# Two-layer graph and expert network on one core: the first layer's expert rows are added into a table in device memory and loaded back in three groups, in place of a table of expert rows and eleven gathers

## The reference, cut to what matters

```python
x = x + graph0(layernorm(x), adj)                 # adj @ (input * W)
x = x + ffn0(layernorm(x))                        # attention, then the first expert layer
x = x + graph1(layernorm(x), adj)                 # attention over the graph, with adj as weights
x = x + ffn1(layernorm(x))                        # second expert layer

# inside ffn0: a normed input x, x = x + attention(x), then with h2 = layernorm(x)
for i in range(8):                                # capacity = ceil(1354 * 1.6 / 8) = 271
    mask = (topk_idx == i).any(-1)                # each token has its two best experts
    sel = first `capacity` tokens of the mask
    yi = gelu(h2[sel] @ w1[i] + b1[i]) @ w2[i] + b2[i]
    out = out.at[sel].set(yi, mode='drop')        # a later expert overwrites an earlier one
return x + out
```

## Time and profile before

| what | value |
|---|---|
| median of three runs | 882.79 us |
| the profiled execution, device time | 877.23 us |
| its span in the profile | 875.4 us |
| TensorE busy | 772.8 us (88%) |
| VectorE busy | 611.6 us (70%) |
| ScalarE busy | 409.9 us (47%) |
| GpSimd busy | 336.2 us (38%) |
| mean granted TensorE clock | 0.944 of full speed |

### The profile page before, as it was taken

One profiled execution on the slowest core, in us unless ns is written; L12 is line 12 of the kernel. 1 busy time (PEld: TensorE's weight loads), 2 busy tenths in 40 slices (PEclk: granted clock), 3 DMA queues, 4 the chain that ended last, 5 costly groups with the idle time before them and its releaser, 6 DMA issues. The chain is left out here.

```text
span 875.4 us, 13715 instructions
## 1 busy us (share of the span) xinstructions
PE 772.8 (88%) x4212; PEld 583.1 (67%) x4213; DVE 611.6 (70%) x1175; ACT 409.9 (47%) x836; POOL 336.2 (38%) x333
## 2 busy tenths in 40 slices
PE   5999888999999999752999992999957999999994
PEld 4997554555555543342999992577846888888883
DVE  6675777766666679984898984687785655666552
ACT  3336344555566556612657552642342454444551
POOL 2700257676666777734252105000002344333332
PEclk9999989999999999985999996999968999999997
DMA  7538776787887777505155402972293287752110
GB/s 270 205 107 323 175 243 230 258 264 250 271 259 257 252 242 233 184 1 200 48 212 176 176 27 62 388 268 92 96 356 102 44 283 230 233 165 37 31 19 0
DMA packets 61623, 159.02 MB, mean 182 GB/s; under 512 B 20875, under 2 KB 39489, under 8 KB 58371
## 3 DMA queue, kind: packets, MB, share of 16 engines
q1 hardware_dynamic: 40627, 97.97, 33.1%
q0 software_dynamic: 20944, 60.38, 22.3%
HBM read 103.00 MB, written 49.93 MB: 175 GB/s over the span
## 5 line engine op out<-in xcount | busy, mean ns | idle before, releaser
L1858 DVE TENSOR_REDUCE mx<-ps 128x1 f32<-128x452 f32 x264 | 148.4, 621 | 68.3 <-PE ps L1314 67.5
L971 ACT ACTIVATE expo<-ps 128x452 f32<-128x452 f32 x264 | 124.5, 551 | 89.7 <-PE ps L1326 88.5
L1334 PE MATMUL ps<-expo,v_st 128*64 128x452 f32 (+1 forms) x576 | 117.3, 529 | 0.0
L1159 ACT ACTIVATE h<-ps,b_l 128x128 f32<-128x128 f32 x224 | 61.0, 384 | 114.6 <-PE ps L1668 111.7
L1314 PE MATMUL ps<-k_st,q_st 96*128 96x452 f32 x264 | 106.0, 413 | 6.8 <-DVE mx L1858 6.5
L1326 PE MATMUL ps<-q_st,k_st 98*128 98x452 f32 x264 | 97.1, 392 | 2.4 <-ACT expo L971 2.3
L905 POOL DMA_INDIRECT out<-y1t,out_row x29 | 46.2, 1592 | 118.2 <-DVE share L2254 94.6
L1314 PEld LDWEIGHTS ps<-k_st,q_st 96*128 96x128 f32 x264 | 50.7, 192 | 53.2 <-DVE mx L1858 36.7
L1685 PE MATMUL ps<-w_ring,h_hi 128*128 x232 | 82.5, 394 | 1.3 <-DVE h_lo L2266 0.5
L837 POOL TENSOR_TENSOR part_lo<-part,part_hi 128x512 fp32r<-128x512 f32 x64 | 80.9, 1289 | 0.5
L2278 DVE COPY h1pre<-ps 128x1024 f32<-128x1024 f32 x29 | 35.5, 1224 | 61.7 <-PE ps L1661 61.6
(11 more groups left out here) (352 smaller groups left out, 1786.3 us busy)
## 6 DMA issues: line engine op xcount, KB each, us to landing
w_l<-w_l SPq DMA_DIRECT2D x8, 2053.0 KB, 8.4
part<-w_l POOLq DMA_DIRECT2D x32, 512.0 KB, 4.9
w_split_d<-part_hi POOLq DMA_DIRECT2D x32, 512.0 KB, 3.8
w_split_d<-part_lo POOLq DMA_DIRECT2D x32, 512.0 KB, 3.7
adj<-adj_t SPq DMA_DIRECT2D x22, 704.0 KB, 4.2
w_ring<-w_split_d SPq DMA_DIRECT2D x10, 1365.5 KB, 7.0
w_ring<-w_split_d SPq DMA_DIRECT2D x5, 1365.0 KB, 6.0
w_ring<-w_split_d SPq DMA_DIRECT2D x1, 4096.0 KB, 13.5
```

The lines of the kernel that those rows point to most:

```text
L971: act.activation(expo[g % 8][:, :], ps[:, 3 + g % 3, 0:QC], ACT.Exp, scale=SCALE).then_inc(s_exp, 1)
L1159: last = act.activation(h1[:, f, :], ps[:, 4 + f // 4, (f % 4) * P:(f % 4 + 1) * P], ACT.Gelu_apprx_tanh, bias=b1_l1[:, bass.ds(e, 1), f])
L1334: return pe.matmul(ps[at:at + 2 * DK, 6 + g // T % 2, lo:hi], v_st[h % 2][:, kt, :], expo[g % 8][:, lo:hi], start=kt < 2, stop=kt == T - 1 ...
L1858: dve.tensor_reduce(mx4[:, n // KB, n % KB:n % KB + 1], ps[:, i % 3, 0:KC], AX_X, ALU.max).then_inc(s_mx, 1)
```

## The change

The sum of residual and u is made before the experts (VectorE, behind `goal0`) and written to a new memory table `x2_d` of 1408 rows. GpSimd adds each expert's rows into that table with three indirect DMAs as soon as ScalarE has copied them, one expert after the other, and tells ScalarE through a new semaphore when a buffer `y0` is free. A list `out_row0` names the destination rows: it comes from `place_of0` with two small instructions, and places without a token point out of range. When all 24 scatters have landed, SP loads `x2_d` back into `x_res` in three DMAs, one for each group, and then the adjacency. The table `ys0_d`, its 16 writes, the eleven gathers, the memset of `nat`, the list `idx` and VectorE's eleven additions are gone. SP no longer waits for an expert's rows between weight loads. TensorE's order is changed: `right(1)` and `left(1)` come before `turn_group(2)`, and `features(0, 2)` behind it.

```diff
 @@ constants and tiles
-GOALS0_READY, ROWS0_NUMBERED, WEIGHTS_READY, GOALS_READY = 1, 2, 3, 4
+GOALS0_READY, WEIGHTS_READY, GOALS_READY = 1, 2, 3
-        idx = place("idx", [T], I32)
+        out_row0 = place("out_row0", [TILES0], I32)
-        x0_d, ys0_d = scratch("x0_d", [P + NP, D]), scratch("ys0_d", [SLOTS0, D])
+        x0_d, x2_d = scratch("x0_d", [P + NP, D]), scratch("x2_d", [NP, D])
-        RIGHT_DONE, LEFT_DONE = (1, 3, 4), (2, 5, 6)
+        RIGHT_DONE, LEFT_DONE = (1, 3, 5), (2, 4, 6)
 @@ SP (behind the write of x0_d, L690)
-            def experts(i, last):
+            sp.wait_ge(s_x2, 1)
+            sp.dma_start(x2_d.rearrange("(t p) d -> p t d", p=P), x_res[:, :, :]).then_inc(s_x2_out, 16)
+
+            with sp.Fori(0, E // 2 - 1) as i:
                 for k in range(2):
                     e = i * 2 + k
-                    if not last:
-                        sp.wait_ge(s_w1lo, e + 1)
-                        sp.wait_ge(s_w2lo, e + 1)
-                        sp.dma_start(w_l0[k][:, :], ...).then_inc(s_w0[k], 16)
-                    sp.wait_ge(s_yo, PRIMED + e + 1)
-                    sp.dma_start(ys0_d[bass.ds(e * CAPP, (CT - 1) * P), :]..., y0[k][:, 0:CT - 1, :]).then_inc(s_ys[k], 16)
-                    sp.dma_start(ys0_d[bass.ds(e * CAPP + (CT - 1) * P, CREM), :], y0[k][0:CREM, CT - 1, :]).then_inc(s_ys[k], 16)
-            with sp.Fori(0, E // 2 - 1) as i:
-                experts(i, False)
-            experts(E // 2 - 1, True)
+                    sp.wait_ge(s_w1lo, e + 1)
+                    sp.wait_ge(s_w2lo, e + 1)
+                    sp.dma_start(w_l0[k][:, :], ...).then_inc(s_w0[k], 16)
+
+            sp.wait_ge(s_ys, 16 * CT * E)
+            for n, (lo, hi) in enumerate(ROW_GROUPS):
+                sp.dma_start(x_res[:, lo:hi, :], x2_d[lo * P:hi * P, :].rearrange("(t p) d -> p t d", p=P)).then_inc(s_x2_in[n], 16)
             sp.wait_ge(s_y0_ps, PRIMED + E)
-            for t in range(T):
-                sp.wait_ge(s_gath[t], 16)
             for j in range(3):
                 sp.dma_start(adj1[j][:, :], adj[j]).then_inc(s_adj1[j], 16)
 @@ GpSimd (behind load_xs0(0) and load_xs0(1))
-            for e in range(2, E):
-                load_xs0(e)
-                if e == ZERO_AT:
-                    pool.memset(nat[:, :, :], 0.0).then_inc(s_gz, 1)
-            pool.wait_ge(s_gz, 1)
-            pool.wait_ge(s_idx, ROWS0_NUMBERED)
-            for k in range(2):
-                pool.wait_ge(s_ys[k], PRIMED + 32 * (E // 2))
-            for t in range(T):
-                pool.indirect_dma_start(
-                    out=nat[:, t, :], out_offset=None, in_=ys0_d[:, :],
-                    in_offset=bass.IndirectOffsetOnAxis(ap=idx[:, t:t + 1], axis=0),
-                    bounds_check=SLOTS0 - 1, oob_is_err=False).then_inc(s_gath[t], 16)
+            def add_rows0(e):
+                pool.wait_ge(s_yo, PRIMED + e + 1)
+                for c in range(CT):
+                    w = P if c < CT - 1 else CREM
+                    at = e * CT + c
+                    pool.indirect_dma_start(
+                        out=x2_d[:, :], out_offset=bass.IndirectOffsetOnAxis(ap=out_row0[0:w, at:at + 1], axis=0),
+                        in_=y0[e % 2][0:w, c, :], in_offset=None, bounds_check=N - 1, oob_is_err=False,
+                        compute_op=ALU.add).then_inc(s_ys, 16)
+
+            for e in range(E):
+                if e + 2 < E:
+                    load_xs0(e + 2)
+                if e == 0:
+                    pool.wait_ge(s_x2_out, 16)
+                else:
+                    pool.wait_ge(s_ys, 16 * CT * e)
+                    pool.sem_inc(s_y_free, 1)
+                add_rows0(e)
 @@ ScalarE, rows_out
-                act.wait_ge(s_ys[k], PRIMED + written)
+                act.wait_ge(s_y_free, PRIMED + added)
 @@ TensorE
             turn_group(1)
+            right(1)
+            left(1)
+            turn_group(2)
             features(0, 2)
-            turn_group(2)
-            right(1)
             right(2)
-            left(1)
             left(2)
 @@ VectorE, before the experts (behind goal0, L1997)
-            slot_numbers(C_OFF)
-            row_number(sa)
+            step(dve.tensor_scalar(beyond0[:, :], place_of0[:, :], 0.0, FAR, ALU.is_equal, ALU.mult))
+            dve.scalar_tensor_tensor(out=out_row0[:, :], in0=place_of0[:, :], scalar=-float(P), in1=beyond0[:, :],
+                                     op0=ALU.add, op1=ALU.add)
+            dve.tensor_tensor(x_res[:, :, :], x_res[:, :, :], u[:, :, :], ALU.add).then_inc(s_x2, 1)
 @@ VectorE, behind the experts
-            dve.tensor_tensor(x_res[:, :, :], x_res[:, :, :], u[:, :, :], ALU.add).then_inc(s_x2, 1)
...
-            dve.wait_ge(s_x2, 1)
             def normed_group(n):
                 lo, hi = ROW_GROUPS[n]
+                dve.wait_ge(s_x2_in[n], 16)
                 for t in range(lo, hi):
-                    dve.wait_ge(s_gath[t], 16)
-                    dve.tensor_tensor(x_res[:, t, :], x_res[:, t, :], nat[:, t, :], ALU.add).then_inc(s_x2, 1)
-                    if t > lo:
-                        dve.wait_ge(s_x2, 1 + t)
-                        dve.bn_stats(stats[:, t - 1, :], x_res[:, t - 1, :])
-                dve.wait_ge(s_x2, 1 + hi)
-                step(dve.bn_stats(stats[:, hi - 1, :], x_res[:, hi - 1, :]))
+                    last = dve.bn_stats(stats[:, t, :], x_res[:, t, :])
+                step(last)
```

More of the change, by code:

```diff
@@ L39 @@
 CREM = CAPP - (CT - 1) * P
-SLOTS0 = E * CAPP
 TILES0 = E * CT
 TILES1 = (2 * N + E * (P - 1)) // P
-GOALS0_READY, ROWS0_NUMBERED, WEIGHTS_READY, GOALS_READY = 1, 2, 3, 4
+GOALS0_READY, WEIGHTS_READY, GOALS_READY = 1, 2, 3
 PAIR_BANKS = (3, 4, 5, 7, 3, 4)
@@ L47 @@
 ZEROED = 48
-ZERO_AT = 4
 B2_BANKS = (3, 3, 4, 4, 5, 5, 6, 6, 1, 1, 2)
@@ L335, in build_program @@
         place_of0 = place("place_of0", [TILES0])
+        beyond0 = place("beyond0", [TILES0])
         assert cursor[0] <= offsets["lg"]
@@ L457, in build_program @@
         s_yo = sem("y0_ready")
-        s_ys = [sem(f"ys0_written{i}") for i in range(2)]
-        s_gz = sem("gather_zeroed")
-        s_gath = [sem(f"rows_gathered{t}") for t in range(T)]
+        s_ys = sem("expert_rows_added")
+        s_y_free = sem("expert_rows_buffer_free")
+        s_x2_out = sem("residual_rows_written")
+        s_x2_in = [sem(f"summed_rows_loaded{n}") for n in range(len(ROW_GROUPS))]
         ROUTER_DONE, BIAS_DONE, WO_TURNED, FOLD_DONE, WAL_DONE, COMB_TURNED = range(1, 7)
@@ L509, in build_program @@
         s_b2 = sem("b2_products_done")
-        s_x2 = sem("two_residuals_added_then_layer0_tile_summed")
+        s_x2 = sem("two_residuals_added")
         s_b2_add = sem("b2_added")
@@ L547, in build_program @@
         PRIMED = 1
-        primed = [s_exp, s_av, s_cr, *s_cout, s_h0, s_hlo, s_y0_ps, s_yt, s_yo_ps, s_yo, *s_ys,
+        primed = [s_exp, s_av, s_cr, *s_cout, s_h0, s_hlo, s_y0_ps, s_yt, s_yo_ps, s_yo, s_y_free,
                   s_g1, s_y1_ps, s_y1, s_ring]
@@ L1031, in _, with rows_out, expert0 @@
             act.activation(std[:, 0:1], ones[:, 0:1], ACT.Gelu)
-            def rows_out(e, k, written):
+            def rows_out(e, k, added):
                 act.wait_ge(s_yo_ps, PRIMED + e + 1)
-                act.wait_ge(s_ys[k], PRIMED + written)
+                act.wait_ge(s_y_free, PRIMED + added)
                 act.activation(y0[k][:, 0:2, :], ps[:, 6, :].rearrange("p (s d) -> p s d", d=D), ACT.Identity)
                 act.activation(y0[k][0:CREM, 2, :], ps[0:CREM, 7, 0:D], ACT.Identity).then_inc(s_yo, 1)
-            def expert0(i, k, first=False, more=True):
+            def expert0(i, k, first=False, reused=True, more=True):
                 e = i * 2 + k
@@ L1047, in expert0 @@
                     if f == YT_AT and not first:
-                        rows_out(e - 1, 1 - k, i * 32 if k else i * 32 - 32)
+                        rows_out(e - 1, 1 - k, i * 2 + k - 2 if reused else 0)
                 if more:
@@ L1058, in _ @@
             expert0(0, 0, first=True)
-            expert0(0, 1)
+            expert0(0, 1, reused=False)
             with act.Fori(1, E // 2 - 1) as i:
@@ L1064, in _ @@
             expert0(E // 2 - 1, 1, more=False)
-            rows_out(E - 1, 1, (E // 2 - 1) * 32)
+            rows_out(E - 1, 1, E - 2)
             def normed_group(n):
@@ L1960, in choose @@
                 step(dve.tensor_tensor(mask[:, :, :], key, over_e(valid), ALU.mult))
[L1962 to L1966, removed]
             for k in range(PARTS_AHEAD):
@@ L1974, in _ @@
             step(dve.tensor_tensor(mask[:, :, :], mask[:, :, :], slot[:, :, :], ALU.mult))
[L1975 to L1981, removed]
+            off = const[:, C_OFF0:C_OFF0 + E].rearrange("p (o e) -> p o e", o=1).to_broadcast([P, T, E])
+            step(dve.tensor_tensor(slot[:, :, :], pos, off, ALU.add))
+            step(dve.tensor_tensor(slot[:, :, :], slot[:, :, :], mask[:, :, :], ALU.mult))
```

(1 more changed line is left out.)

8 lines of the change are left out of this document (2 added, 6 removed).

## The result

With the change four runs took 906.31, 899.20, 906.67 and 903.22 us, a median of 904.76 us, against 881.96 us for the kernel before (its three runs and one more beside these). The ratio on record is 1.029 with a 95% interval of 1.023 to 1.034; the two medians by themselves stand 22.8 us or 2.6% apart. Of the twelve executions of all_group2 further down, one was over 1.5% above that kernel's fastest and is left out of its median and ratio. The sign was forecast, the size was not: 890.4 us and a range to 897 us.

What follows compares the result with a forecast made beforehand. TensorE was taken as full during the experts, so only the ends could change: head +2.8, experts 0, tail +4.8, sum +7.6 us on the profiled 877.2 us, or 890.4 us on the median 882.8; range 885 to 897 us.

Steps and rivals of the forecast that it cites:

- The head's addition: Ahead of the experts: VectorE's big addition holds GpSimd's first gather, +2.1 us, bounds 0 and 3.1.
- The rival built on the sentence of the Trainium skill: Head: the addition does not stop the gathers, only the tail's 4.8 us remain, 887.6 us; chance 0.22.
- The head's traffic: Head: third gather lands amid the x2_d write and expert 2's weights, +0.7 us, between 0 and 0.8.
- The experts: Expert stage: GpSimd gathers later and weight loads leave earlier, yet TensorE never waits; 0 us.
- Cover: Experts: expert 3's gathers land at 448.5, TensorE turns them at 449.99, leaving 1.5 us.
- The queue order that was forecast: Experts: on GpSimd, the gathers of expert e + 3 come behind expert e's scatters; 0 us, thin cover.
- GpSimd's queue comes late: Experts: rival that slower scatters make TensorE wait up to 1 us for each of five experts, 895.4 us; chance 0.15.
- The tail: Behind the experts: end of right(2) comes 4.8 us later, 1.4 from the later start and 3.4 from the order.
- First turn of group 0: Tail: scatters and new loads make group 0's turn on TensorE start 1.4 us later, bounds +0.5 and +2.5.
- order +3.4 forecast: Tail: TensorE's new order, with left(1) in front and new gaps, delays the end of right(2) by 3.4 us.
- ScalarE's copy: Tail: ScalarE copies features 0 and 1 before group 2, so TensorE waits 1.3 us before right(2).
- The faster rival: Tail: the last gather sets the end, so group 2's earlier load gains up to 4.4 us, 878.4 us; chance 0.06.

Runs made afterwards that it cites:

- all_group2: all_mended plus group 2 normed before group 0's maximum (VectorE) and group 1's copies (ScalarE); median 883.2 us, ratio 1.0021 to the kernel before.
- write_late: weights_first plus a wait, so the write of x2_d leaves once expert 0's rows are turned; goal0 to first turn 8.3 us, whole run 886.8 us.
- add_late: weights_first with the addition, then the write of x2_d, behind the split of expert 0's rows; goal0 to first turn 6.2 us, whole run 897.6 us.
- weights_first: Changed kernel with expert 2's weights sent ahead of SP's wait for the sum; goal0 to first turn 10.5 us, whole run 894.7 us.
- gather_first: Changed kernel with GpSimd gathering expert e + 3 ahead of expert e's scatter; expert stage 119.5 us, whole run 902.5 us.
- weights_paced: Changed kernel with weight loads again waiting for the rows of the expert before; expert stage 120.2 us, whole run 886.3 us.
- old_pe_order: Changed kernel with TensorE's old order of the groups restored; last expert rows to end of right(2) 29.8 us, whole run 899.2 us.
- act_copy_first: Changed kernel with ScalarE copying group 2 ahead of features 0 and 1; last expert rows to end of right(2) 31.9 us, whole run 905.6 us.
- before_add_head: Kernel before with only VectorE's addition of u moved directly behind goal0; goal0 to first turn 8.0 us, whole run 880.6 us.
- all_mended: Changed kernel with gather_first, weights_first, add_late and old_pe_order joined; median 882.1 us over 12 runs, ratio 1.0025 to the kernel before.

## Why the prediction was wrong

**The head's addition: right.** Forecast +2.1 us by the pattern of a gather begun inside a two-operand subtraction, measured 2.1 (write_late against add_late) and 2.0 in isolation. The rival built on the sentence of the Trainium skill, "SBUF — State Buffer", section "Who interferes with whom", that a `tensor_tensor` leaves descriptor generation alone, fails: the gather took 3.00 and 3.30 us against 1.09. The page's other sentence, that two SBUF inputs contend with a GpSimd instruction that reads SBUF, agrees with the rows.

**The head's traffic: the step that failed.** The prediction said that the third gather "lands in that traffic" and priced it between 0 and 0.8 us, from one gather that had met a weight load 5 us old. Here the load was 1.8 us old when the third gather began. weights_first and write_late show 4.8 + 2.2 = 7.0 us in place of the 0.7 taken. The term was mis-sized by a factor of ten: a small gather behind a fresh 2053 KB load lands only about when the load does. The row that I took could not show it, as its gather landed at 445.0, 1.8 us behind the load's end at 443.2. The two gathers in front of it in the same trace show it (442.9 and 443.9).

The Trainium skill, page "DMA: Bandwidth & Descriptors", section "Queues, rings and completion order", says that each DMA engine takes turns between its queues by whole packets of many descriptors. By that alone I would expect a small gather to be through well before a big load ends. The traces show it landing with the load: 0.8 us before the end of the weights in the head (422.83 against 423.67), and 0.2 us behind their end in the experts (466.0 against 465.8). Whether its data or only its completion is held back, no run here separates.

**The experts: the step that failed.** "The weight loads start some microseconds earlier, at the low halves, and are not waited for either way." Nobody waits for them, but one now left while the gathers of expert 3 were being issued, and these had no slack. Cover was worked out as 1.5 us with a landing 2.2 us behind the end of a gather's issue, from the row of an old load; with a fresh one the third gather landed 6.7 us behind it. The queue order that was forecast is real, and so is the rival "GpSimd's queue comes late", but its price and its cause were wrong: not slower scatters at 1 us for each expert, but two collisions, at experts 3 and 5, with 3 us of waiting each and then half clock on TensorE. The half clock was in no term of the sum: 3.8 of the 9.9 us. Scatters that slow VectorE's splits are not the cause, as X is at its old value in gather_first and weights_paced with all scatters in place.

**The tail: right.** First turn of group 0 +1.4 forecast, +1.2 measured; order +3.4 forecast, +3.5 measured by old_pe_order; ScalarE's copy 1.3 forecast, 1.24 in the row and 1.3 by act_copy_first. The loads landed as those of the kernel's start did (3.9, 4.9, 5.5 against 3.6, 4.6, 6.5).

**The faster rival** (the last gather sets the end) is refuted: with group 2 loaded early and normed early, all_group2 gains at most 0.7 us.

## What to carry to other kernels

When a plain load is released from a wait, look which small transfers will leave just behind it, even on another engine's queue: their landing goes from 3 us to the end of the load (7.5 to 9.4 us after their start here). Price a collision by when the big transfer will land, not by any row in which the two overlap: look at every gather near such a load in the trace, also at those that nobody waits for. A stall of 3 us on TensorE cost the stall and then some half clock behind it here, so a thin cover deserves a case of its own in the forecast, with both terms.

## What the runs showed of the hardware that was not expected

- A gather of 16 rows begun 1.0 to 1.8 us behind the issue of a 2053 KB load on SP's queue landed 7.5 to 9.4 us after its start (changed kernel and gather_first), with 2.3 to 2.4 us when no load was under way. In each of these rows it landed between 1.2 us before and 0.2 us behind the end of the load; in weights_first gathers landed in the same way with the end of the 1408 KB write of `x2_d`.
- A gather begun while VectorE added or subtracted two SBUF operands for 2.28 or 3.08 us ended 0.8 to 1.0 us after VectorE's instruction in every such row of the kernel before, the changed one, before_add_head, write_late, gather_first, weights_paced and all_mended. One begun 0.02 to 0.03 us into a subtraction of 0.8 us took its usual 1.0 us (kernel before, five times).
- Each of the two waits of about 3 us in the changed kernel came with the granted clock at half, for 3.4 us behind the first (window at 0.88) and for 6.8 us around and behind the second (windows at 0.79 and 0.96): 5.2 us of full speed beside 6.1 us of waiting.
